# Decoder layer on one core: cross-attention key bias multiplied on Pool, stack memsets ahead of the first root, four warm-up products, side pieces of the loop in new places

## The reference

```python
x = x + attn(layernorm(x))      # causal, rotary, 32 query heads, 8 key/value heads of 16
x = x + xattn(layernorm(x), ctx)
x = x + ffn(layernorm(x))       # three ternary weights

# xattn: one head of 512 features, 512 context tokens per sequence
Q = text @ Wq.T + bq
K = ctx @ Wk.T + bk
attended = softmax(Q @ K.T / sqrt(512)) @ ctx

# each weight w of ffn (1376 x 512, one 512 x 1376)
scale = mean(abs(w)); q = round(clip(w / (scale + 1e-5), -1, 1)); w = q * scale
out = (h @ gate.T * (h @ up.T)) @ down.T
```

## Time and profile before

| | us |
|---|---|
| median of 3 runs | 243.01 |
| the three runs | 239.43, 243.01, 243.68 |
| the profiled execution | 241.45 |
| its span in the trace | 239.7 |

### The profile page before, as it was taken

The page is one execution under the profiler, slowest core; times in us unless marked ns, Lnnn a source line. Parts: engine busy times, 40 slices in busy tenths (PEclk is TensorE's granted clock), DMA queues, the critical chain, the costliest instruction groups (busy, mean ns, idle before and its releaser), DMA issues.

```text
span 239.7 us, 4254 instructions
## 1 busy us (share of the span) xinstructions
PE 226.2 (94%) x1470; PEld 163.2 (68%) x1478; DVE 153.3 (64%) x562; ACT 125.4 (52%) x208; POOL 43.0 (18%) x65
## 2 busy tenths in 40 slices
PE   7699988999999999999999997999999999999994
PEld 2359867777767777546774553787877778767771
DVE  2549978996797699579361558976557565353323
ACT  2636786666679657465587263834643223323230
POOL 2692000272133224122301022010000000000000
PEclk9689999999999999999999999999999999999999
DMA  6999300000345321440811081000000000020002
GB/s 154 379 396 410 124 1 1 2 4 1 122 127 173 100 50 45 131 162 17 294 49 44 3 285 66 0 3 0 3 1 0 0 3 0 0 90 1 3 0 88
DMA packets 9077, 19.97 MB, mean 83 GB/s; under 512 B 1152, under 2 KB 1536, under 8 KB 9056
## 3 DMA queue, kind: packets, MB, share of 16 engines
q1 hardware_dynamic: 8480, 19.60, 23.6%
q10 hardware_dynamic: 576, 0.10, 0.2%
HBM read 18.58 MB, written 1.05 MB: 82 GB/s over the span
## 4 chain that ended last, share of the span: by engine, by line
PE 75%; DVE 12%; DMA 4%; issue 3%; ACT 2%; SPq 1%; POOL 1%; DVEq 0%; ACTq 0%; POOLq 0%
PE ps L1278 16%; PE ps L1293 8%; PE ps L1143 7%; PE ps L1216 4%; PE ps L1169 4%; PE ps L1122 4%; PE ps L1076 4%; PE ps L1091 3%; PE ps L1200 3%; PE ps L1231 3%; PE ps L1374 3%; DVE ps L969 3%; DMA raw<-down_dram 3%; PE ps L1388 2%; PE ps L1345 2%
## 5 line engine op out<-in xcount | busy, mean ns | idle before, releaser
L969 DVE CUSTOM_DVE_ANT_0 ps<-ps,maskf 128x128 f32<-128x128 f32 (+1 forms) x128 | 41.0, 392 | 1.9 <-PE ps L1338 1.8
L511 POOL TENSOR_SCALAR_AFFINE_SELECT prob<-prob 128x512 f32<-128x512 f32 x32 | 20.1, 652 | 86.2 <-ACT prob L727 86.2
L727 ACT ACTIVATE prob<-ps 128x1536 f32<-128x1536 f32 x16 | 23.2, 1451 | 15.2 <-PE ps L1377 15.2
L596 ACT CAST in_hi<-inter 128x256 f16<-128x256 f32 (+1 forms) x22 | 8.9, 405 | 23.9 <-DVE inter L931 23.9
L1278 PE MATMUL ps<-h_hi,gate_q 128*128 128x256 f16 (+1 forms) x88 | 20.4, 273 | 0.0
L1278 PE MATMUL ps<-h_hi,up_q 128*128 128x256 f16 (+1 forms) x88 | 20.4, 273 | 0.0
L1278 PE MATMUL ps<-h_lo,up_q 128*128 128x256 f16 (+1 forms) x88 | 20.4, 272 | 0.0
L1278 PE MATMUL ps<-h_lo,gate_q 128*128 128x256 f16 (+1 forms) x88 | 20.4, 272 | 0.0
L931 DVE TENSOR_TENSOR inter<-gate_s,ps 128x256 f32<-128x256 f32 (+1 forms) x22 | 9.2, 419 | 16.5 <-PE ps L1278 15.4
L466 POOL TENSOR_TENSOR rstd<-veps,neghalf 128x1 f32<-128x1 f32 x12 | 7.5, 623 | 66.8 <-DVE veps L760 66.8
L969 DVE DVE_READ_ACCUMULATOR2_ANT mx<- 128x1 f32 x128 | 17.8, 139 | 0.0
(11 more groups left out here) (172 smaller groups left out, 502.3 us busy)
## 6 DMA issues: line engine op xcount, KB each, us to landing
raw<-gate_dram SPq DMA_DIRECT2D x1, 2752.0 KB, 17.1
raw<-up_dram SPq DMA_DIRECT2D x4, 688.0 KB, 4.1
wqkv<-wqkv_dram SPq DMA_DIRECT2D x4, 384.0 KB, 6.8
raw<-down_dram SPq DMA_DIRECT2D x2, 768.0 KB, 4.8
x<-x_dram SPq DMA_DIRECT2D x4, 256.0 KB, 6.3
xwq<-xwq_dram SPq DMA_DIRECT2D x1, 1024.0 KB, 9.3
xwk<-xwk_dram SPq DMA_DIRECT2D x1, 1024.0 KB, 11.3
wo<-wo_dram SPq DMA_DIRECT2D x1, 1024.0 KB, 18.2
```

The costliest lines, as they stand in the source:

```text
L511: nc.gpsimd.affine_select(out=v, in_=v, compare_op=ALU.is_ge, fill=0.0, base=0, pattern=[[0, GROUP], [1, P]], channel_multiplier=-1).then_ ...
L727: nc.scalar.activation(prob[:, i % 2, :], ps[:, 3:6, :].rearrange("p a b -> p (a b)"), ACT.Exp, scale=DH ** -0.5).then_inc(exp_done, 1)
L969: nc.vector.tensor_tensor_reduce(scores, scores, mask, 1.0, LOWEST, ALU.add, ALU.max, to).then_inc(max_done, 1)
```

## The change

The pieces `u` no longer multiply with a spread bias. Pool multiplies each of the four row blocks of `xwq` by its bias column and adds them up (four multiplications and three additions of 128 x 512, tile `bkq`, the terms in the place of `oT`), and TensorE sums over the partitions with one product with `ones` for each piece. `bqbc` shrinks to 32 columns. Pool's stack memsets stand ahead of `root(0)`. There are four warm-up products. Pool does seven `whole` chunks and not three. Most side pieces, three loads and a column sum get other places.

```diff
-WARM_UP = 3
+WARM_UP = 4
-        bkbc = sb("bkbc", [P, KD, P])
-        bqbc = sb("bqbc", [P, KD, P])
+        bkq = sb("bkq", [P, D])
+        bqbc = sb("bqbc", [P, KD, 32])
+        bkq_term = oT[:, :, :].rearrange("p a q -> p (a q)")
+        bkq_set = sem("bkq_set")
-        POOL_CHUNKS = [(0, 0), (0, 1), (1, 1)]
+        POOL_CHUNKS = [(0, 0), (0, 1), (0, 2), (0, 3), (1, 0), (1, 3), (2, 1)]
         BESIDE = [
-            ([], [("abs", 0, 1), ("abs", 0, 2)], [("pq", 3)]),
-            ([("abs", 0, 3)], [("rot", 3, 0)], [("pk", 3), ("st", 10), ("hi", 3, 0)]),
-            ([("hi", 3, 1), ("rot", 3, 1)], [("a", 0, 0), ("part", 0)], [("st", 11)]),
-            ([("lo", 3, 0), ("lo", 3, 1)], [("st", 12)], [("whole", 0, 0), ("a", 0, 1), ("whole", 0, 1),
-             ("tern", 0, 0), ("whole", 0, 2)]),
-            ([("st", 13)], [("st", 14), ("tern", 0, 1)], [("a", 1, 0)]),
-            ([("st", 15)], [("whole", 0, 3), ("st", 16)], [("tern", 0, 2), ("a", 1, 1)]),
-            ([("st", 17)], [("tern", 0, 3), ("st", 18)], [("st", 19)]),
-            ([("abs", 1, 0)], [], [("abs", 1, 1), ("a", 2, 0)]),
-            ([], [], [("abs", 1, 2), ("u", 0)]),
+            ([("abs", 0, 1)], [("pq", 3)], [("abs", 0, 2)]),
+            ([("abs", 0, 3)], [("pk", 3), ("rot", 3, 0), ("st", 10)], []),
+            ([("st", 11), ("part", 0), ("whole", 0, 0)], [("hi", 3, 0), ("a", 0, 0)], [("st", 12), ("rot", 3, 1),
+             ("hi", 3, 1)]),
+            ([], [("lo", 3, 0)], [("lo", 3, 1), ("a", 0, 1), ("whole", 0, 1), ("tern", 0, 0)]),
+            ([("st", 13)], [("st", 14), ("whole", 0, 2), ("tern", 0, 1)], [("a", 1, 0), ("tern", 0, 2)]),
+            ([("st", 15)], [("st", 16)], [("whole", 0, 3), ("a", 1, 1)]),
+            ([("st", 17)], [("st", 18)], [("tern", 0, 3), ("abs", 1, 0), ("st", 19)]),
+            ([], [], [("a", 2, 0), ("abs", 1, 1)]),
+            ([], [("u", 0)], [("abs", 1, 2)]),
             ([("abs", 1, 3)], [("part", 1)], [("u", 1)]),
             ([], [], [("c",)]),
-            ([("whole", 1, 0), ("whole", 1, 1)], [("cc", 0), ("tern", 1, 0)], [("whole", 1, 2), ("a", 2, 1)]),
-            ([("whole", 1, 3)], [("cc", 1)], [("wo", 0), ("tern", 1, 1)]),
-            ([("tern", 1, 2)], [("wo", 1), ("tern", 1, 3)], [("n2", 0), ("a", 3, 0), ("n2", 1), ("xT", 1, 0)]),
-            ([], [("low", "wo", 0), ("xT", 1, 1)], [("a", 3, 1)]),
-            ([("high", "wo", 0), ("high", "wo", 1), ("abs", 2, 0), ("g", 0, 0), ("abs", 2, 1), ("low", "wo", 1)],
-             [("high", "wo", 2)], [("abs", 2, 2), ("g", 0, 1), ("high", "wo", 3), ("abs", 2, 3), ("abs", 2, 4)]),
-            ([("xs", 0)], [("part", 2), ("low", "wo", 2)], [("xs", 1), ("xpT", 0)]),
-            ([], [("whole", 2, 0), ("low", "wo", 3)], [("xpT", 1), ("xo", 0), ("whole", 2, 1), ("n3", 0)]),
-            ([("tern", 2, 0), ("xo", 1)], [], [("tern", 2, 1), ("xT", 2, 0)]),
-            ([("n3", 1), ("hl", 0), ("cc", 2)], [("xT", 2, 1)], [("whole", 2, 2), ("tern", 2, 2), ("whole", 2, 3),
-             ("whole", 2, 4), ("hl", 1)]),
+            ([], [("cc", 0)], [("a", 2, 1), ("whole", 1, 0)]),
+            ([("whole", 1, 1), ("whole", 1, 2)], [("tern", 1, 0)], [("whole", 1, 3), ("wo", 0)]),
+            ([("cc", 1)], [("wo", 1), ("tern", 1, 1)], [("tern", 1, 2), ("n2", 0), ("a", 3, 0)]),
+            ([("xT", 1, 0), ("n2", 1)], [("tern", 1, 3)], [("a", 3, 1), ("low", "wo", 0), ("high", "wo", 0),
+             ("xT", 1, 1)]),
+            ([("abs", 2, 0), ("g", 0, 0), ("high", "wo", 1), ("low", "wo", 1)], [("abs", 2, 1), ("high", "wo", 2)],
+             [("low", "wo", 2), ("abs", 2, 2), ("g", 0, 1)]),
+            ([("abs", 2, 3), ("abs", 2, 4), ("xs", 0)], [("part", 2)], [("xs", 1), ("xpT", 0)]),
+            ([("whole", 2, 0)], [("low", "wo", 3)], [("whole", 2, 1), ("xpT", 1), ("xo", 0)]),
+            ([("high", "wo", 3), ("tern", 2, 0), ("n3", 0), ("xo", 1)], [], [("tern", 2, 1)]),
+            ([("xT", 2, 0), ("n3", 1), ("hl", 0)], [("cc", 2), ("xT", 2, 1)], [("whole", 2, 2), ("whole", 2, 3),
+             ("tern", 2, 2), ("hl", 1), ("whole", 2, 4)]),
         ]
...
-        COLUMN_AT = {10: ("sum", 1), 17: ("sum", 2), 3: ("sum", 0), 12: ("dot",)}
+        COLUMN_AT = {17: ("sum", 2), 3: ("sum", 0), 11: ("sum", 1), 12: ("dot",)}
-        ST_ON_ACT = (10, 12, 14, 16, 18)
-        UP_LOADS, CTX_LOAD, DOWN_LOADS = {4: (0,), 5: (1,), 6: (2,), 7: (3,)}, 8, {11: (0,), 12: (1,), 13: (2, 3)}
+        ST_ON_ACT = (10, 12, 14, 16, 18, 19)
+        UP_LOADS, CTX_LOAD, DOWN_LOADS = {3: (0,), 5: (1, 2), 6: (3,)}, 6, {11: (0,), 12: (1, 2), 13: (3,)}
-            root(0)
             for s in range(2):
                 nc.gpsimd.memset(stk[:, s, :, 0, :], 0.0).then_inc(stack_set, 1)
             pool.wait_ge(stack_set, 2)
             for s in range(2):
                 nc.gpsimd.memset(stk[:, s, HEADS:HEADS + KV, 0, 0:1], -1.0).then_inc(stack_set, 1)
+            root(0)
-            nc.gpsimd.tensor_copy(bkbc[:, :, :], bqk[:, 1, :].unsqueeze(2).broadcast_to([P, KD, P])
-                                  ).then_inc(bkbc_set, 1)
+            pool.wait_ge(xw_in, 32)
+            nc.gpsimd.tensor_scalar(bkq[:, :], xwq[:, 0, :], bqk[:, 1, 0:1], None, ALU.mult).then_inc(bkq_set, 1)
+            for k in range(1, KD):
+                nc.gpsimd.tensor_scalar(bkq_term, xwq[:, k, :], bqk[:, 1, k:k + 1], None, ALU.mult
+                                        ).then_inc(bkq_set, 1)
+                pool.wait_ge(bkq_set, 2 * k)
+                nc.gpsimd.tensor_tensor(bkq[:, :], bkq[:, :], bkq_term, ALU.add).then_inc(bkq_set, 1)
+                pool.wait_ge(bkq_set, 2 * k + 1)
+                    if i == 0:
+                        act.wait_ge(bkq_set, 2 * KD - 1)
                     elif kind == "u":
-                        for k in range(KD):
-                            mm = nc.tensor.matmul(to[:, 0:T], bkbc[:, k, :], xwq[:, k, arg[0] * T:(arg[0] + 1) * T],
-                                                  start=(k == 0), stop=(k == KD - 1))
+                        pe.wait_ge(bkq_set, 2 * KD - 1)
+                        mm = nc.tensor.matmul(to[:, 0:T], ones[:, :], bkq[:, arg[0] * T:(arg[0] + 1) * T],
+                                              start=True, stop=True)
```

More of the change, by code:

```diff
@@ L491, in _ @@
             nc.gpsimd.memset(maskf[:, 0:P], 0.0).then_inc(bkbc_set, 1)
-            nc.gpsimd.tensor_copy(bqbc[:, :, :], bqk[:, 0, :].unsqueeze(2).broadcast_to([P, KD, P])
+            nc.gpsimd.tensor_copy(bqbc[:, :, :], bqk[:, 0, :].unsqueeze(2).broadcast_to([P, KD, 32])
                                   ).then_inc(bkbc_set, 1)
-            nc.gpsimd.tensor_copy(bkbc[:, :, :], bqk[:, 1, :].unsqueeze(2).broadcast_to([P, KD, P])
-                                  ).then_inc(bkbc_set, 1)
+            pool.wait_ge(xw_in, 32)
[6 more added lines that the diff above has]
+                pool.wait_ge(bkq_set, 2 * k + 1)
             def side(pieces):
@@ L1402, in output_T @@
                 mm.then_inc(oT_ps, 1)
-            pe.wait_ge(bkbc_set, 3)
+            pe.wait_ge(bkbc_set, 2)
             pe.wait_ge(consts_set, 3)
```

16 lines of the change are left out of this document (8 added, 8 removed).

## The result

The changed kernel took 237.93 us (median of 4 executions, 237.75 to 238.41) against 241.59 for the kernel before in the same sitting (4 executions, 239.43 to 243.68). The ratio is 0.990, its 95% interval 0.985 to 0.995: faster by 1%, less than the 2% from which this measurement calls a kernel faster. The ratios here compare fast executions alone, those within 1.5% of the fastest one of the same kernel, and so the quotient of the two medians (0.985) is not the ratio. Executions of one kernel scatter by up to 7 us.

The account below looks back on a forecast made before the run. TensorE, busy 226.2 of 239.7 us, was taken as the bound. Terms summed to -4.3 us, 0.4 given back: 237.55, then half way towards the 243.01 median: 238.3; range 236.2 to 240.4, 8 in 10 between 234.0 and 242.0.

Parts of the forecast that it names:

- `u`, -1.1 us: Loop steps 8 to 10: shorter `u` saves 0.57 + 0.71 us; the moved column sum costs some 0.15.
- the ring: Loop steps with `u`: row maxima, scores by key and transpose wait on each other, a floor of 4.28 us a step.
- The fourth warm-up and the memsets, 0: Start: transposes 0.84 us earlier, warm-up costs 0 to 0.6; Pool's `w_lo` until 18.06 us lets little arrive.
- The front, +0.25 taken as 0: Before the loop: L798 done 1.25 us earlier, VectorE loses 1.5 us to Pool's additions; bounds -2.1 and +5.5.
- Pool's chain, 6.7 us: Front, on Pool: four multiplications at 0.62 and three additions at 1.21 us, with waits 6.7, until about 25.5 us.
- R1: Front: Pool's chain holds the port through its waits, L798 is 5.5 us late, 245.3 us in all; chance 0.07.
- First steps, -0.8: Loop's first steps: of 1.78 us of gaps, 0.59 closed for `st` 12 and 0.2 for the next maxima.
- 100 to 116 us, -0.6 and -0.2: Loop steps from 100.22 and 115.80 us: 0.6 of 0.69 us of gap closed, and 0.2 of 0.30 by the earlier load.
- R2: Whole loop: the new order opens as many gaps as it closes, 241.1 us; chance 0.25.
- The loop's end, -1.4: Steps from 142.48 and 148.42 us: 1.4 of 0.78 + 1.16 us of gaps closed by reordering around `ctx_tok`; bounds 0 and 1.9.
- AFTER, 0: The part AFTER: TensorE has next to no gap there, so 0; bounds -0.5 and +1.
- signs of being wrong: Steps 8, 9 above 4.6; second transpose stack over 1 us past 27.4 or before 25.3; TensorE waits over 1 us, steps 11-19.

Follow-up runs that it names:

- the kernel with the earlier load: The kernel before with the second half of the last load of `down` issued one group earlier (after group 12, not 13), nothing else: ratio 0.9983.
- the three kernels whose gap ahead of the first transpose is 1.12 to 1.25 us: Changed kernel with Pool waiting between third and fourth `w_lo`, 0.9949; with Pool's key-bias chain behind the front, 0.993; with both and `abs` (1, 3) moved, 0.9912.
- the last two edits together: Changed kernel with Pool waiting between third and fourth `w_lo`, two-operation key-bias chain behind front, `abs` (1, 3) behind `u` 1, `part` 1 later: 0.9912.

## Why the prediction was right, and what in it was wrong

The number (238.3 for 237.93), the range and the likeliest class (within 2%) held, and the number by luck, as the terms show: most of them were off, and their errors cancelled. Against the kernel before of the same sitting the gain is 1.0%, not the 1.9% that the text gives: the median of 3 runs shown, 243.01, was high by 1.4 us against the 4 of that sitting and by 2.9 against the 96 later ones. The step half way towards that median was a wrong correction that did not hurt: without it the forecast, 237.55, would have been as near. The terms, in the prediction's order:

- **`u`, -1.1 us.** Measured -0.76 across the three steps. Its step 8 fell to the 4.28 us of the ring, as said. The next stayed at 4.56: TensorE waits 0.80 us for the copy `oT`, which ScalarE does behind `abs` (1, 3). "It fits" was the step that failed: ScalarE had 4.32 us of work there and not 3.58, as the end of the absolute sum before runs over into this step, and the copy stood behind the next one. With `abs` behind the copy ScalarE has 3.58 and the step takes 4.28. The piece takes 0.70 us, not 0.48. The column sum cost 0.24, not 0.15.
- **The fourth warm-up and the memsets, 0.** Right in the changed kernel, where taking back either changed nothing. The reason given, that Pool's `w_lo` sets the front, is half of it: seven fronts take 20.46 to 20.50 us from the third `w_lo`, whatever TensorE does, but with the whole old start at full clock two profiles show 19.10 and 19.33. There VectorE's addition gets in between the two `w_lo`. And in the kernel before both edits cost 1 us.
- **The front, +0.25 taken as 0; -1.89 in the two profiles.** The size came from what the sum left out. Pool's third `w_lo` began 0.69 us earlier (13.74 for 14.43), with the load of x and not through an edit. The other 1.20 is the way from that `w_lo` to the loop, 20.47 us against 21.67 in the profiled execution before. That execution ran its front at half clock; the same instructions at full clock, in the kernel with the earlier load, take 19.10. "I put the clock at 0" was thus wrong against that execution. Against the kernel before at full clock the term was too kind: with 19.10 and 19.33 in two profiles, the changed kernel's front is 1.1 to 1.4 us longer. Its L808 is shut out by both `w_lo`.
- **Pool's chain, 6.7 us; 11.8 measured.** The step that failed is the price of the multiplications: "the nearest row" was a copy at 0.62, and `tensor_scalar` with one operation takes 1.56. Additions were right (1.21 forecast, 1.28). At 1.56 and 1.28 the seven make 10.1 us; the rest are waits between them and 1.3 us that three of them lost beside VectorE. Of the four to five collisions expected two came: L820 lost 0.1 us beside a multiplication and then 1.1 beside an addition, but L808 and L817 at 18.79 and 19.08 ran at 0.29 and 0.69 inside a multiplication. The rival R1 (the port stays shut through the chain) was wrong: VectorE got in again and again. What it feared did come in another place, between two `w_lo` without a wait.
- **First steps, -0.8.** Measured -0.10: step 3 became 0.46 longer (5.88) and step 4 0.57 shorter. The exponential of group 0 starts at 39.38, right behind its scores, as said, but both stack transposes in one step only moved the work. The gaps from 31 to 45 us stayed at 1.77, and TensorE's waits of 0.52 and 0.46 us for ScalarE in it stand as they stood: the step that failed is that a freed ScalarE would close them.
- **Around 65 us, -0.2.** -0.13 up to the 8th transpose.
- **100 to 116 us, -0.6 and -0.2.** -0.42 in one step and -0.36 in the other, and -0.58 in the one before; but the step from 106.50 takes 6.75 where 5.43 was, so that all five give -0.03. TensorE's gaps in them went from 0.99 to 0.82 us: 0.17 closed where 0.8 was forecast, and its own work grew by 0.14. The wait of 0.46 us that stood in the step from 100.22 now stands in the one from 106.50, which also holds more pieces. This is near R2 ("opens as many gaps as it closes").
- **The loop's end, -1.4.** Measured -0.73. The wait of 0.78 for `ctx_tok` at 147.08 is gone, the second one became 0.49, and a new one of 0.49 for `oT` appeared at 144.65.
- **AFTER, 0.** -0.26.

So the sum was near, by luck, because a front that was sized at 0 gave 1.9 in these two profiles, while the loop gave 1.75 (0.23, 0.76, 0.03 and 0.73) where 4.3 were written down. R2 came nearer to what the loop did. None of the signs of being wrong that the prediction names appeared: its steps 8 and 9 took 4.28 and 4.56 us, the second stack of transposes started at 25.50, and no new wait of TensorE of over 1 us came in steps 11 to 19. They were set too wide to catch this.

What the whole change does then, by the experiments: it takes 0.8 us through the order (with the load of `down`) and some 0.9 through `u` in that order, about 2 us in all for the two variants that have both, against the kernel before of the same sitting. Taking back one of the start's edits changes nothing; both at once were not taken back. Its clock also seems to fall less often. Executions with a mean granted clock below 0.996: changed kernel 0 of 4, its variants with the old bias 0 of 12, the old memsets 1 of 10, three warm-ups 4 of 11, the order alone 2 of 12; the kernel before 38 of 96, with the earlier load 5 of 12, with four warm-ups 3, with the memsets 1, with both 6; 9, 9 and 3 of 12, 12 and 6 in the three kernels whose gap ahead of the first transpose is 1.12 to 1.25 us, 11 of 12 in the one with the bias alone (1.12 us). That such a gap causes the fall is argued, from these counts and from the order of events in the profiles (the last section has them); it is not shown. Against it: the kernel with the memsets alone, whose profile has a gap of 1.47 us and the fall behind it, was at 0.997 or more in its 11 other executions, and 6 of 12 were low with both start edits, whose profile has a gap of 0.78 us ahead of the first transpose (and one of 1.30 in step 16, with no fall behind it).

Open: why VectorE's addition gets in between Pool's two subtractions in some kernels and not in others. With 1.84 us for the third `w_lo`, it arrived 0.45, 0.19 and 0.12 us ahead of the end of that one where it got in (the earlier load, the order, the bias alone), and 0.29 to 0.39 ahead in the eight kernels where it didn't: no rule of arrival fits all. All three that got in have the whole old start, three warm-up products and the memsets behind the root; of the eight every one has at least one of the start's edits. So the start may cost what it is thought to bring, some 1.2 us, and only the changed kernel without both edits could tell. Against it: order with start (0.9952) was no slower than the order alone (0.9968). Whether one kernel can do both was not seen, as each has one profile; the executions at full clock of the kernel with the earlier load, 237.77 for the profiled one and 239.4 to 240.2 for four others, suggest it.

## What to carry to other kernels

Cost the engine's order, not its load: a piece that fits a step by the sum of its times can still delay the one copy that TensorE waits for. A second engine's helper work is free only where it doesn't stand beside the last two-input operations of VectorE ahead of a wait; put Pool's chains either well before or well behind that, and look at which form of the instruction is fast. Before a start is tuned, find what the front's length is counted from (here Pool's third subtraction): edits ahead of that point didn't arrive in this kernel.

## What the runs showed of the hardware

- **Pool's multiplication.** `tensor_scalar` with one operation, 128 x 512 by a column: 1.56 us; with a second operation (add 0.0): 0.69, at another time and, for three of the four, into another tile. A copy of 128 columns spread from four took 0.30 where it ran undisturbed (the last two edits together) and 0.61 to 0.82 in the other kernels, beside VectorE; one of 512 took 0.62.
- **The shared port.** VectorE's addition with both inputs in SBUF, starting 0.12 to 0.45 us ahead of the end of Pool's third `w_lo`, came out only behind the fourth in eight kernels (2.70 to 2.77 us), and between them in three (0.69 to 1.02); so it did in the two where Pool was made to wait (0.95 and 1.01). The Trainium skill, page "SBUF — State Buffer", section "Who interferes with whom", says that whoever issues first gets the pair for the whole instruction. By that rule L808, which the profile starts before the fourth `w_lo`, should always come ahead of it; the eight kernels show that back to back instructions of Pool can keep the pair. The kernel before shows it with its two copies, too (L798 from 18.34 to 19.85).
- **Not every read of Pool shuts it out.** The same section of the Trainium skill lets an operation of VectorE with two SBUF inputs contend with any GpSimd instruction that reads SBUF. Here an addition cost VectorE up to 1.1 us (1.37 for 0.28) and a multiplication in the two-operation form 0.4 (0.70 for 0.28), as that says, while L808 and L817 ran at 0.29 and 0.69 inside the slow multiplication at 18.10. The slow form isn't free of VectorE, though: one that started at 22.68, 0.12 us behind an L808 of 0.69 us, took 2.01 us and not 1.56.
- **The clock.** The granted clock fell to 0.50 behind gaps of TensorE of 1.12 and 1.14 us (both with the bias alone), 1.25 and 1.47 us. It also did so in two profiles near 82 us, behind the wait of 0.80 us for `oT`. It did not behind gaps of 1.12, 1.20, 1.30 and 1.38 us in four other profiles, nor behind the same wait of 0.80 us in three (the changed kernel among them). Ahead of the first transposes it was 0.50 behind a gap of 1.96 us and stayed at 1.00 behind one of 1.43 in the kernel with the earlier load. The length of a gap alone doesn't tell. A stretch at 0.50 lengthened a step by 1.2 to 3.4 us (5.67 for 4.52, 9.29 for 5.88).
